# Square sums of half the up weights: from products on TensorE to pieces on ScalarE, in an attention and mixture-of-experts kernel

## The reference, cut to what matters

```python
kv = k_v @ W_k.T + b_k                      # k_v: context, 512 x 128 a batch
out = einsum('bij,bjd->bid', p, kv)         # p = layernorm(x)
sim = einsum('bid,bjd->bij', out, kv) * scale
sim = (sim - mu) * rsqrt(var + EPS) * ln_gamma + ln_beta
x = x + softmax(sim)
n = layernorm(x)
scores = einsum('btd,ed->bte', n, Wg); top 2 of 8, softmax over the two
y += w[..., e:e+1] * einsum('bth,dh->btd', silu(n @ W1[e].T) * (n @ W2[e].T), W3[e])
x = x + y
```

## Time and profile before

| | |
|---|---|
| median of 3 runs | 391.74 us (391.63 to 392.01) |
| the profiled execution | 392.64 us, of which its span in the profile is 390.9 us |
| PE busy | 363.9 us (93%) |
| DVE, ACT, POOL busy | 246.4 (63%), 230.9 (59%), 165.3 us (42%) |
| products of the weight Gram matrices | 176 |

### The profile page before, as it was taken

The page is one execution under the profiler, slowest core; times in us unless marked ns, Lnnn a source line. Parts: engine busy times, 40 slices in busy tenths (PEclk is TensorE's granted clock), DMA queues, the critical chain, the costliest instruction groups (busy, mean ns, idle before and its releaser), DMA issues.

```text
span 390.9 us, 8201 instructions
## 1 busy us (share of the span) xinstructions
PE 363.9 (93%) x2340; PEld 243.5 (62%) x2340; DVE 246.4 (63%) x625; ACT 230.9 (59%) x406; POOL 165.3 (42%) x194
## 2 busy tenths in 40 slices
PE   6889899988997899999999999999999999999981
PEld 5555667667985555656666666666666666666640
DVE  1266758878285967562566676757666676757660
ACT  1246756646231999883657566666657566666650
POOL 2116666685923022435434434352534434352421
PEclk9999999995559999999999999999999999999998
DMA  6998999868962124335445353545445353535423
GB/s 207 409 415 312 310 408 350 317 195 341 277 215 63 46 27 84 59 61 100 78 86 89 75 103 64 107 62 101 78 88 87 77 101 66 106 61 105 74 36 54
DMA packets 22121, 57.61 MB, mean 147 GB/s; under 512 B 4864, under 2 KB 4992, under 8 KB 20544
## 3 DMA queue, kind: packets, MB, share of 16 engines
q0 software_dynamic: 8736, 20.53, 29.7%
q1 hardware_dynamic: 11184, 20.17, 14.7%
q10 hardware_dynamic: 2160, 16.38, 11.2%
HBM read 38.17 MB, written 18.91 MB: 146 GB/s over the span
## 4 chain that ended last, share of the span: by engine, by line
PE 74%; issue 8%; POOL 7%; ACT 3%; DVE 3%; DMA 3%; POOLq 1%; ACTq 0%; DVEq 0%
PE bank L1260 34%; PE bank L1281 15%; PE bank L1271 5%; PE bank L1251 4%; PE bank L1303 3%; PE bank L1104 3%; PE bank L1125 2%; PE bank L1028 1%; ACT Wp L625 1%; PE bank L1159 1%; PE bank L1147 1%; DMA out<-kvj_s,sidx 1%; POOL vr L421 1%; POOL rstd L424 1%; DMA ng_s<-n_table,gidx 1%
## 5 line engine op out<-in xcount | busy, mean ns | idle before, releaser
L1260 PE MATMUL bank<-Wp,kvg_s 128*128 x480 | 78.3, 313 | 1.9 <-DVE kvg_s L971 1.8
L1260 PE MATMUL bank<-Wp,kv_s 128*128 x456 | 74.3, 313 | 1.2 <-DVE kv_s L971 1.0
L965 DVE SCALAR_TENSOR_TENSOR stage<-W,w3sc,stage 128x512 f16<-128x512 f16 x93 | 66.9, 747 | 7.2 <-ACT stage L660 7.2
L1281 PE MATMUL bank<-stage,n_s 128*128 128x512 f16 (+1 forms) x279 | 65.3, 379 | 1.5 <-issue 1.5
L1260 PEld LDWEIGHTS bank<-Wp,kvg_s 128*128 128x128 f16 x480 | 46.7, 98 | 29.6 <-issue 5.3
L517 POOL DMA_INDIRECT out<-oT_s,sidx x20 | 31.9, 1593 | 76.2 <-ACT oT_s L691 69.0
L660 ACT ACTIVATE stage<-W,w3sc 128x512 f16 x93 | 63.2, 717 | 0.0
L1260 PEld LDWEIGHTS bank<-Wp,kv_s 128*128 128x128 f16 x456 | 44.4, 98 | 27.3 <-issue 4.3
L517 POOL DMA_INDIRECT out<-kvj_s,sidx x19 | 30.1, 1585 | 66.7 <-ACT kvj_s L691 64.0
L992 DVE TENSOR_TENSOR n_s<-bank,n_s 128x384 f16<-128x384 f32 x31 | 17.3, 558 | 51.8 <-ACT n_s L673 51.8
L501 POOL DMA_INDIRECT ng_s<-n_table,gidx x39 | 38.9, 998 | 25.4 <-issue 11.3
(11 more groups left out here) (188 smaller groups left out, 562.2 us busy)
## 6 DMA issues: line engine op xcount, KB each, us to landing
Wp<-in_w ACTq DMA_DIRECT2D x7, 1408.0 KB, 9.2
W<-in_w ACTq DMA_DIRECT2D x8, 768.0 KB, 5.5
W<-in_x SPq DMA_DIRECT2D x12, 256.0 KB, 9.5
out<-W SPq DMA_DIRECT2D x12, 256.0 KB, 6.2
stage<-in_xT SPq DMA_DIRECT2D x2, 1024.0 KB, 6.6
Wp<-in_xT SPq DMA_DIRECT2D x2, 1024.0 KB, 8.9
n_table<-n_s SPq DMA_DIRECT2D x8, 256.0 KB, 4.1
n_table<-x_s SPq DMA_DIRECT2D x8, 256.0 KB, 5.4
```

What stands on the lines that cost most here:

```text
L965: eng.scalar_tensor_tensor(w3p[r][:, W3N + c * D:W3N + (c + 1) * D], W3[:, bass.ds(e * W3N + c * D, D)], w3sc[:, bass.ds(e, 1)], w3p[r][:, ...
L1260: mm = eng.matmul(bank[2 * which + r][:, 0:H], n_, w_, start=(c == 0 and k == 0), stop=(c == DC - 1 and k == 2))
L1281: mm = eng.matmul(ybank(t)[:, :], h_, w_, start=(c == 0 and k == 0), stop=(c == HC - 1 and k == 2))
```

## The change

Experts 0, 2, 4 and 6 keep their Gram products, in slots (1, 2), (3, 4), (7, 8) and (11, 12), 11 products to a slot. For experts 1, 3, 5 and 7 ACT squares the float32 weights in four pieces of 128 x 704 with a sum each, into the new array wsqa, in the slots of PIECE_SLOTS. A piece stands directly behind Exp in ACT's slot, except in slots 3, 7, 11 and 15, where it stands at the end. Slot 13 has two pieces, slot 15 too. weight_norms gets four more products with ones, one for each piece index, and waits for all 16 pieces. PE's 12 products with ones, until now in slots 15 and 16, are there in slots 13 to 16; the wait for the last diagonal moves from slot 15 to slot 13. DVE has four diagonals fewer and two small memsets more, at the start. For experts 1, 3, 5 and 7 the scale then comes from the full float32 weights, not from their upper 16 bits.

```diff
--- before.py
+++ after.py
@@ -58,7 +58,9 @@
 WARM_GATHER = 20
 WARM_ROWS = 6
 WARM_SLOT = 12
-GRAM_SLOTS = ((1,), (2,), (3, 4), (5, 6), (7, 8), (9, 10), (11, 12), (13, 14))
+GRAM_SLOTS = {0: (1, 2), 2: (3, 4), 4: (7, 8), 6: (11, 12)}
+PIECES = 4
+PIECE_SLOTS = {1: (2, 3, 4, 5), 3: (6, 7, 8, 9), 5: (10, 11, 12, 13), 7: (13, 14, 15, 15)}
 WARM_START = 48
 NSCALE = 2.0 ** 10
 WSCALE = 2.0 ** 15
@@ -134,6 +136,8 @@
         minus1 = sb("minus1", [P, TPB])
         wsq = sb("wsq", [P, E])
         diag = sb("diag", [P, P])
+        wsqa = sb("wsqa", [P, PIECES, E])
+        junkw = sb("junkw", [P, W12N // PIECES], BF16)
         wsum = sb("wsum", [P, E])
         wrs = sb("wrs", [P, E])
         wrec = sb("wrec", [P, E])
@@ -232,6 +236,7 @@
         s_wg, s_wq, s_wqp, s_wmax, s_wrs, s_wsc, s_wrec, s_winv = [
             sem(n) for n in ("s_wg", "s_wq", "s_wqp", "s_wmax", "s_wrs", "s_wsc", "s_wrec", "s_winv")]
         s_hi, s_lo = sem("s_hi"), sem("s_lo")
+        s_wqa, s_wqz = sem("s_wqa"), sem("s_wqz")
         s_w3q, s_w3qp, s_w3s, s_w3r, s_w3sc, s_w3rec, s_yinv, s_yt = [
             sem(n) for n in ("s_w3q", "s_w3qp", "s_w3s", "s_w3r", "s_w3sc", "s_w3rec", "s_yinv", "s_yt")]
         s_w3h, s_w3l = sem("s_w3h"), sem("s_w3l")
@@ -583,6 +588,8 @@
                     wait(eng, s_ei, g - 1)
                     eng.activation(L_s[:, k, :], L_s[:, k, :], ACT.Exp, scale=-1.0, bias=lmin[:, k:k + 1],
                                    accum_out=esum[:, k:k + 1]).then_inc(s_E, 1)
+                if i != 2:
+                    weight_pieces(n)
                 if i == 2 and real(b + 1):
                     gram_copy(b + 1)
                     o_evac(b + 1)
@@ -600,9 +607,23 @@
                     kv_evac(b + 2)
                 if i == 0 and real(b + 1):
                     kvj_evac(b + 1)
+                if i == 2:
+                    weight_pieces(n)
                 if n == 20:
                     w12_high(0, 0)
                     w12_high(0, 1)
+
+            def weight_pieces(n):
+
+                for e, slots in PIECE_SLOTS.items():
+                    for j, s in enumerate(slots):
+                        if s == n:
+                            eng.wait_ge(s_w[e], 16)
+                            eng.wait_ge(s_wqz, 2)
+                            wait(eng, s_wqa, PIECES * (e // 2) + j)
+                            m = W12N // PIECES
+                            eng.activation(junkw[:, :], wst[e][:, j * m:(j + 1) * m], ACT.Square,
+                                           accum_out=wsqa[:, j, e:e + 1]).then_inc(s_wqa, 1)
 
             def w3_square(k):
                 e = W3_ORDER[k]
@@ -804,7 +825,8 @@
 
             def diagonal(k):
 
-                eng.wait_ge(s_wg, k + 1)
+                eng.wait_ge(s_wg, k // 2 + 1)
+                eng.wait_ge(s_wqz, 1)
                 eng.tensor_tensor_reduce(diag[:, :], bank[5][:, P:2 * P], ident[:, :], 1.0, 0.0, ALU.mult, ALU.add,
                                          wsq[:, k:k + 1]).then_inc(s_wq, 1)
 
@@ -848,7 +870,7 @@
                     if i < TPB - 1:
                         scale_in(bn_, in_)
                 n = TPB * (b + 1) + i - (TPB - 1)
-                for k in range(E):
+                for k in GRAM_SLOTS:
                     if n == GRAM_SLOTS[k][-1] + 1:
                         diagonal(k)
                 if real(b):
@@ -893,6 +915,8 @@
             eng.memset(spare_v[:, 12:13], 0.0).then_inc(s_scp, 1)
             eng.memset(spare_v[:, 13:14], 0.0).then_inc(s_scp, 1)
             eng.memset(spare_v[:, 15:16], 0.0).then_inc(s_ti, 1)
+            eng.memset(wsq[:, :], 0.0).then_inc(s_wqz, 1)
+            eng.memset(wsqa[:, :, :], 0.0).then_inc(s_wqz, 1)
             eng.wait_ge(s_const, NCONST)
             eng.tensor_copy(steps8[:, :, :], iota[:, :, None].to_broadcast([P, P, TPB * TOPK])).then_inc(s_eoff, 1)
             eng.tensor_copy(tok16[:, :, :], tok1[:, :, None].to_broadcast([P, G, TOPK])).then_inc(s_eoff, 1)
@@ -1135,13 +1159,17 @@
 
             def weight_norms(n):
                 eng.wait_ge(s_msq, B)
-                eng.wait_ge(s_wq, E)
-                eng.matmul(bank[1][:, E:2 * E], ones[:, :], wsq[:, :], start=True, stop=True).then_inc(s_wqp, 1)
+                eng.wait_ge(s_wq, E // 2)
+                eng.matmul(bank[1][:, E:2 * E], ones[:, :], wsq[:, :], start=True, stop=False)
+                eng.wait_ge(s_wqa, E // 2 * PIECES)
+                for j in range(PIECES):
+                    mm = eng.matmul(bank[1][:, E:2 * E], ones[:, :], wsqa[:, j, :], start=False, stop=(j == PIECES - 1))
+                mm.then_inc(s_wqp, 1)
 
             def weight_gram(k, first, last):
 
                 eng.wait_ge(s_w[k], 16)
-                wait(eng, s_wq, k)
+                wait(eng, s_wq, k // 2)
                 for c in range(first, last):
                     w_ = upper[k][:, c * P:(c + 1) * P]
                     mm = eng.matmul(bank[5][:, P:2 * P], w_, w_, start=(c == 0), stop=(c == W12N // P - 1))
@@ -1202,17 +1230,16 @@
                     keys(b + 2)
                 if i == 0 and real(b + 1):
                     turn_keys(b + 1)
-                if n > GRAM_SLOTS[E - 1][-1]:
-                    if n == 2 * E - 1:
-                        eng.wait_ge(s_wq, E)
+                if n > GRAM_SLOTS[E - 2][-1]:
+                    if n == GRAM_SLOTS[E - 2][-1] + 1:
+                        eng.wait_ge(s_wq, E // 2)
                     warm(ones16[:, :], WARM_SLOT)
-                for k, slots in enumerate(GRAM_SLOTS):
+                for k, slots in GRAM_SLOTS.items():
                     if n in slots:
                         h, part = slots.index(n), W12N // P // len(slots)
                         weight_gram(k, h * part, (h + 1) * part)
                 turn_n(*lag(b, i, 2))
                 if n == 15:
-                    eng.wait_ge(s_wq, E)
                     table(0)
                     table(1)
                 if i == 1 and real(b + 1):
```

## The result

The changed kernel takes 396.5 us (395.2 to 397.6, 4 runs) against 391.7 us for the kernel before (391.5 to 392.0, 4 runs beside it): ratio 1.0121, 95% interval 1.0085 to 1.0157. It is slower, as forecast, by 4.8 us in the median where 2.7 were forecast. The profiled execution took 395.20 us, with a span of 393.4: 2.6 us more than the profiled execution of before (392.64), close to the sum of the prediction. Another part of the loss comes in some executions and not in others. The four runs stand in two pairs, 395.2 and 395.8, 397.3 and 397.6.

The account below looks back on a forecast made before the run. PE was taken as nearly full, with ACT's latency on a second path almost as long that leads in slots 13 to 15. Terms 0 + 0 + 1.0 + 1.7 = +2.7 us gave 394.5 us, range 391.2 to 397.8.

Parts of the forecast that it names:

- Four summing products: Slot 16 on PE: four more products at half clock, in series with nothing hiding them, +1.7 us; lower end 0.9.
- Turn of tile 12: Slots 13 to 15: pieces delay ACT's row squares and POOL's row, so PE turns tile 12 at 94.5, +1.0 us.
- A piece: One 704-column square on ACT takes 0.80 us, range 0.68 to 0.86; the read of the sum overlaps the next start.
- Slots 1 to 4: Tile 1 comes about a microsecond earlier, and the pieces of slots 2, 3 and 4 use that up: 0.
- Slots 5 to 12: Scaled of slot 8 0.6 us later, of slot 12 0.55; slot 9 even or half a microsecond late, PE's gain gone.
- second path: ACT's latency, with POOL waiting for its row squares: a path almost as long as PE's, leading in slots 13 to 15.
- Last pieces of slot 15: Two pieces end at 98.4, PE asks for the sum at 100.6: cover 2.2 us, so they cost nothing.
- PE's idle times: PE waits for ACT some 2 us before the rank products near 63 us and 1.5 to 2 before the turn near 85.
- The ends of the terms: Pieces -0.5 to +0.3, turn -1.0 to +0.5, products -0.9 to 0 us; likeliest case given 392.6 to 396.
- rival 2: Clock falls sooner, after 2.5 us of PE idle near 62 us, slowing slots 9 and 10: 397 us; chance 15%.
- Rival 1: PE is the bound all through and ACT's pieces are hidden: -1.3 us, 390.4 us; chance 13%.
- Rival 3: Clock is higher at the end, 98 to 111 us, about 3 us come back: 391.5 us; chance 6%.

Follow-up runs that it names:

- experiment 8: The run pieces_last: the kernel after with every piece at the end of ACT's slot; 394.24 us, ratio 1.0065.
- idle_filled: The kernel after with products with ones in PE's idle time, 32 in slot 5 and 24 in slot 9; 395.13 us, ratio 1.0067.
- no_pieces: The kernel after without ACT's 16 pieces, the square sums of experts 1, 3, 5 and 7 replaced by a constant; 395.43 us, ratio 1.0047.
- sums_alone: The kernel before with only the four more summing products of slot 16, over an array of zeros; 393.98 us, ratio 1.0057.
- before_bridge: The kernel before with 36 instead of 20 products with ones ahead of the first gathered rows; 392.11 us, ratio 0.9998.
- before_filled: The kernel before with products with ones ahead of the turns of slots 13 (20), 14 and 15 (14 each); 392.94 us, ratio 1.0021.
- pieces_alone: The kernel before with only the 16 pieces on ACT, all Gram products kept and PE waiting for no piece; 397.52 us, ratio 1.0141.
- one_sum: The kernel after with one summing product over 40 columns and one DVE reduction, instead of five products; 395.57 us, ratio 1.0084.
- experiment 9: The run idle_filled, 395.13 us; its slot 5 to 9 time is compared with the kernel after, one_sum and after_bridge.
- last_one_sum: The kernel after with every piece at the end of ACT's slot and one summing product; 392.59 us, ratio 1.0021.
- pieces_last: The kernel after with every piece at the end of ACT's slot, behind scaled and row squares; 394.24 us, ratio 1.0065.
- after_bridge: The kernel after with 36 instead of 20 products with ones ahead of the first gathered rows; 395.87 us, ratio 1.0069.

## Why the prediction was right, and where it was not

**The sum.** +2.7 us was forecast, and the profiled execution shows 2.6. That the two are so near is in part luck, twice over. The profile of the kernel after starts 0.53 us earlier than that of before; counted from the first turn of keys the loss is 3.0. And the term of the turn of tile 12 came out only because the clock fell. By its steps:

- *Four summing products: 1.7.* Measured 1.71 in the kernel after and 1.70 alone. Right.
- *Turn of tile 12: +1.0.* Measured +0.8, or +1.34 counted from the first turn of keys. What it waits for is right: POOL's row (2.32 us), behind row squares that the pieces push back, and experiment 8, which takes the pieces from ahead of them, has this wait at 0.21. The stations on the way were, as they stand and counted from the first turn: scaled of tile 13 +1.40 and +1.93 (forecast +1.62), of tile 14 +1.62 and +2.15 (+1.87), the row +1.67 and +2.20 (+1.87). But the size leans on the fall of the clock. In idle_filled, with the same pieces and the clock held in slots 5 to 8, the same three are at +0.71, +0.93 and +0.98 counted so, and the turn at +0.11. By that profile the sum would have been 0.1 + 1.8 = 1.9 us.
- *A piece: 0.80.* Measured 0.784 on average over the 16, and 0.77 to 0.79 from the start of one to the start of the next step. The estimate by the Trainium skill ("ScalarE: Activation LUTs"), 0.77, and my 0.80 both lie within 0.02 of it. Read of the sum included, it costs nothing more, as assumed, but for the two slots with two pieces: there the second starts 0.98 us behind the first (85.72 and 86.70), as it waits until the first is counted as done. The pair of slot 13 took 1.77 instead of 1.6 us.
- *Slots 1 to 4: 0.* Measured: -0.24, made up of -1.19 (no_pieces against before) and +0.95 (after against no_pieces). The two did cancel nearly.
- *Slots 5 to 12.* I had the scaled of slot 8 late by 0.6 and that of slot 12 by 0.55. In the profile they are at 61.41 and 83.54, 0.20 and 0.14 late. The profile started 0.53 us earlier, and counted from the first turn of keys they are 0.73 and 0.67 late. But this agreement is luck: the fall of the clock near 45 us, which I did not have in this case, is in it. Without it (idle_filled), counted from slot 1, scaled of slot 8 comes 0.48 us earlier than in the kernel before and that of slot 12 0.55 earlier, and slot 9's turn of keys 0.76 earlier. I had all of them even or late, and I had named just this, scaled of slots 8 and 12 earlier, as the sign that the second path is not what I took it for. In these slots it is not: part of PE's gain does come through. From slot 13 on it is as I had it: scaled of tile 14 stands 1.48 us later against that of tile 12, forecast were 1.32.
- *Last pieces of slot 15: covered.* The last sum is there at 98.44, PE asks for it at 100.9. Right.
- *PE's idle times.* I expected some 2 us ahead of the rank products near 63 us and 1.5 to 2 us ahead of the turn near 85. Measured are 1.26 us at 62.91, and none at 86.11, where the products with ones ran at half clock until the turn.
- *The ends of the terms.* They add up to -2.4 and +0.8 us, so on the scale of the median 392.1 to 395.3; the 392.6 to 396 of the prediction is nearer to the scale of the profiled execution.

**The median.** The forecast was 394.5, measured are 396.5, inside the range and near the figure of rival 2. But rival 2 as I wrote it did not come: its idle time near 62 us is 1.26 us and not 2.5, and the granted clock is 1.00 from 60 to 79 us. What came is its kind of loss at another place, and my 15% for such a fall was too low. The fall comes in slot 5, near 45 us, in the profiles of all five kernels that leave the pieces behind Exp and the idle time ahead of slot 5 unfilled (idle 1.96 to 1.97 us); it doesn't come in before, sums_alone, before_bridge and before_filled (1.41 to 1.42 us and 11 Gram products behind). The step that failed is the sentence "I enter 0" for slots 1 to 4: in time it was nearly right, but I did not ask what the pieces of slots 3 and 4 do to PE's idle time there, and so put the clock of slots 5 to 8 at nothing, where it costs 1.2 to 3.6 us. This idle time grew from 1.42 to 1.97 us, and I wrote of that very row that PE keeps its clock. The Trainium skill, "TensorE: Matmul & The Clock Gate", says that PE goes back to the lower clock when it waits between bursts; idle_filled, in which the idle time is down to 0.17 us and the clock stays at 1.00, agrees.

**Rival 1** (PE is the bound) is refuted by pieces_alone: +5.8 us with PE's work unchanged, of which the profile shows 0.95 in slots 1 to 4 at full clock. By the best run of no_pieces PE's removed work is worth about 1.6 us, of the 3.8 in the bare sum. **Rival 3** (a higher clock at the end) did not come in the kernel after: 0.50 in 98 to 103 us, as before. It came by parts in one_sum and was worth 1.1 us there.

**What stays open.** Which falls of the clock make up the 2 us between forecast and median is not settled run by run, since only one execution of each kernel is profiled. Two places are shown: slot 5 (1.2 to 3.6 us) and the tail, which in the profile of the kernel after is one of the two shortest, and up to 2.2 us longer in others (the first gathered rows take 1.7 us more in the profiles of six kernels, two of them the kernel before with a small edit on PE). Either is large enough for the 2 us; the profile of the kernel after has the mildest fall of the three compared in experiment 9 and the short tail, and it is the fastest of its four runs. Filling the first place narrowed the spread (last_one_sum 5.3 us, filled 2.2); filling the second did not. In no_pieces, pieces_last and last_one_sum the idle time ahead of slot 5 is 1.4 to 1.5 us with no Gram products behind; the clock fell in two of three, and pieces_last and last_one_sum do the same work in the same order up to there. So neither the idle time nor the products behind it settle it alone. Filling also both shortens the idle time and gives PE more products; idle_filled doesn't tell the two apart. The differences between the medians of the kernel after, one_sum, after_bridge and idle_filled are within their intervals; only their traces tell them apart.

## What to carry to other kernels

An engine that is idle 40% of the time can still lie on the path: look at who waits for its next result, and put added work behind the instructions that others wait for, not ahead of them; here the same 16 squares cost 2.3 us less in the median at the end of the slot. Count the small collecting work that a split brings (five products instead of one), and look at whether its place is in series. And work taken from TensorE can lengthen the rest by its clock: where the profile shows idle time at full clock (here 1.4 us, which grew to 2.0), ask what makes it longer, and judge by many runs: with the idle time filled the spread fell from 5.3 to 2.2 us while the median stayed. Last, when a profile agrees with the sum, check the steps in between as well, counted from a common point: here a gain that I had left out and a fall of the clock that I had left out nearly cancelled.

## What the runs showed of the hardware that I had not expected

The granted clock fell behind an idle time of PE of only 1.40 us with no Gram products after it (no_pieces, 0.83 in 44 to 54 us), and held behind 1.42 us with 11 products of 128 columns after it (before). The same work in the same order up to slot 5 kept the clock in one profile (pieces_last, idle 1.52 us, 1.00) and lost it in another (last_one_sum, 1.53 us, 0.83). A fall near 45 us costs up to 3.6 us in a stretch of 20. The idle time at the first gather (2.06 us in before, 2.09 in sums_alone) is followed by first expert products of 1.96 us in one profile and 3.70 in another, without any piece on ACT too (sums_alone, before_filled). With the 36 products with ones ahead of it, which take 3.16 to 4.02 us, this makes tails of 289.6 to 291.8 us behind the same point of the program, so that a single profile cannot tell two kernels apart to better than about 2 us.
